# Driving terms of states 12 to 15 made with the tokens on the partitions, scaled by ScalarE and turned back by TensorE

## The reference

```python
def step(hst, inp):
    u_i, dt_i, b_i, c_i = inp
    dA = jnp.exp(dt_i[..., None] * A)
    hst = dA * hst + (dt_i * u_i)[..., None] * b_i[:, :, None, :]
    y = jnp.einsum('bkdn,bkn->bkd', hst, c_i)
    return (hst, y)
```

## Time and profile before

| what | value |
|---|---|
| median of 3 runs | 12155.8 µs (12155.32 to 12169.84) |
| span of the profiled execution | 12166.4 µs |
| VectorE busy | 11096.6 µs, 91% |
| GpSimd busy | 9763.2 µs, 80% |
| TensorE busy (matmuls) | 8645.9 µs, 71% |
| ScalarE busy | 7723.7 µs, 63% |

### The profile page before, as it was taken

The page is one execution under the profiler, slowest core; times in us unless marked ns, Lnnn a source line. Parts: engine busy times, 40 slices in busy tenths (PEclk is TensorE's granted clock), DMA queues, the critical chain, the costliest instruction groups (busy, mean ns, idle before and its releaser), DMA issues. The chain is left out here.

```text
span 12166.4 us, 118425 instructions
## 1 busy us (share of the span) xinstructions
PE 8645.9 (71%) x25368; PEld 2428.9 (20%) x25368; DVE 11096.6 (91%) x7359; ACT 7723.7 (63%) x11653; POOL 9763.2 (80%) x4212
## 2 busy tenths in 40 slices
PE   8866666666666666666666666666666666488888
PEld 2321111111111111111111111111111111133333
DVE  7769999999999999999999999999999999866565
ACT  6766666666666666666666666666666666455555
POOL 0029999999999999999999999999999999711210
PEclk9977777777777777777777777777777777698989
DMA  3358877887778887787877788778777888643441
GB/s 107 112 152 182 182 182 181 182 182 183 181 182 182 182 181 183 182 182 178 184 182 182 178 186 182 182 176 185 182 182 178 188 184 184 157 102 91 105 103 48
DMA packets 569247, 2013.70 MB, mean 166 GB/s; under 512 B 82135, under 2 KB 87031, under 8 KB 553975
## 3 DMA queue, kind: packets, MB, share of 16 engines
q1 hardware_dynamic: 565490, 2005.63, 71.1%
q10 hardware_dynamic: 3076, 0.97, 0.1%
...
## 5 line engine op out<-in xcount | busy, mean ns | idle before, releaser
L858 POOL TENSOR_TENSOR dBu<-rep,shared 128x1024 f32<-128x1024 f32 x3072 | 7165.7, 2363 | 837.4 <-DMA rep<-dd_dram 830.8
L641 PE MATMUL py<-hC,fold 128*32 128x512 f32 x12288 | 2966.4, 863 | 2450.5 <-POOL hC L865 1908.2
L818 DVE TENSOR_TENSOR_SCAN pd<-pd,dBu 128x1024 f32<-128x1024 f32 x2048 | 4670.5, 2281 | 16.5 <-issue 6.9
L689 ACT ACTIVATE pd<-rep,a_now 128x1024 f32<-128x1024 f32 x3072 | 3419.6, 1113 | 929.5 <-DVE hC L826 739.4
L826 DVE TENSOR_TENSOR hC<-pd,shared 128x1024 f32<-128x1024 f32 x2048 | 2507.5, 1224 | 160.0 <-DVE pd L818 26.3
L865 POOL TENSOR_TENSOR hC<-h,shared 128x1024 f32<-128x1024 f32 x1024 | 2408.1, 2352 | 242.1 <-DVE h L818 240.9
L818 DVE TENSOR_TENSOR_SCAN h<-pd,dBu 128x1024 f32<-128x1024 f32 x1024 | 2333.3, 2279 | 24.2 <-ACT pd L689 24.2
L701 ACT ACTIVATE carry<-pd 128x1 f32<-128x1 f32 x1536 | 262.0, 171 | 2072.0 <-DVE hC L826 2054.3
L641 PEld LDWEIGHTS py<-hC,fold 128*32 128x32 f32 x12288 | 522.8, 138 | 4666.8 <-POOL hC L865 2770.2
L610 PE MATMUL pp<-xdbl,w_dt 38*96 38x512 f32 x1024 | 714.8, 832 | 371.8 <-ACT xdbl L718 369.3
L599 PE MATMUL pp<-u,w_x 96*38 96x512 f32 x1024 | 670.0, 817 | 338.3 <-DVE RL L801 303.5
...
...
## 6 DMA issues: line engine op xcount, KB each, us to landing
rep<-dd_dram SPq DMA_DIRECT2D x1024, 768.0 KB, 12.1
shared<-bc_dram SPq DMA_DIRECT2D x2048, 256.0 KB, 8.8
u<-u_dram SPq DMA_DIRECT2D x128, 768.0 KB, 5.3
dd_dram<-LG SPq DMA_DIRECT2D x256, 384.0 KB, 4.8
dd_dram<-RL SPq DMA_DIRECT2D x256, 384.0 KB, 3.0
y_dram<-y SPq DMA_DIRECT2D x256, 384.0 KB, 11.6
...
```

The costliest lines, as they stand in the source:

```text
L641: last = mm(py[32 * g:32 * g + 32, t2(t)], fold[:, :], hC[:, j % 2 * 3 + g, t2(t)], start=(j % 4 == 0), stop=(j % 4 == 3), skip_group_chec ...
L689: go(pd[:, i % 2, :], rep[:, half, 0, g, :], ACT.Exp, scale=a_now[:, i:i + 1]).then_inc(S.exped, 1)
L818: v.tensor_tensor_scan(turned(dst, k), turned(pd[:, i % 2, :], k), turned(dBu[:, i % 4, :], k), 0.0, ALU.mult, ALU.add).then_inc(S.scanned, 1)
L858: nc.gpsimd.tensor_tensor(dBu[:, i % 4, :], rep[:, half, 1, g, :], BC[:, s, 0, r, :], ALU.mult).then_inc(S.dbu, 1)
```

## The change

Tiles of r = 3 get their dBu in another way, and are neither driven by GpSimd nor weighed by VectorE.

- The triples are put in another order: `TRIPLES` places both triples of r = 3 side by side, as tiles 9 to 14. Tiles 0 to 8 are r = 0 to 2 of the first half, tiles 15 to 23 r = 0 to 2 of the second.
- TensorE turns the rows of B (`turn_b`) and `delta*u` (`turn_du`) so that the tokens lie on the partitions, in eight blocks of 128. ScalarE copies them out (`copy_b`, `copy_du`), and multiplies each block with the B of its tokens, one state at a time, as a scale per partition (`scale_du`, 32 instructions on 128 x 192 a chunk). TensorE turns the products back (`turn_back`, eight transposes a tile) into a slot of `pd`.
- dA of those tiles goes to `hs` in SBUF, three slots, and the scan runs there in place; the saved state is the scan's first value instead of a fold. All six are weighed by GpSimd, which drives 18 tiles a chunk instead of 24 and weighs 12 instead of 8. VectorE weighs 12 instead of 16.
- `hs`, the turned arrays and B and C share the space that held two copies of B and C. There is one copy of each now, loaded row group by row group (`load_b`, `load_c`, 28 transfers instead of 16).
- The small steps move: `absolute` to `log` of half 0 and of half 1 stand one to two turns earlier, `copy_delta` in turns 8 and 18 instead of 10 and 21, `delta_u` behind tiles 9 and 19 instead of 12 and 23, `copy_x_dbl` in turn 23, `copy_y` in turns 3 and 15. `turned` in names of the code also means "run backwards" (`turned(row, k)`), as before.

```diff
+        turned_dbu = a.shared[:, 0:6 * T].rearrange("p (q g j d) -> p q g j d", q=TB, g=6, j=J)
+        turned_du = turned_dbu[:, :, :, J - 1, :]
+        BB = a.shared[:, 6 * T:9 * T].rearrange("p (r t) -> p r t", r=3)
+        hs = a.shared[:, 9 * T:12 * T].rearrange("p (g t) -> p g t", g=3)
+        CC = a.shared[:, 12 * T:16 * T].rearrange("p (r t) -> p r t", r=4)
...
+        TRIPLES = ((0, 0), (0, 1), (0, 2), (0, 3), (1, 3), (1, 0), (1, 1), (1, 2))
+        DRIVEN, WEIGHED, TURNED, SCALED = 18, 12, 6, 4 * TB
...
+            def turn_du(m, half):
+                pe.wait_ge(S.delta_made, done(m * 2 + half + 1))
+                pe.wait_ge(S.du_made, done(m * 2 + half + 1))
+                for q in range(TB):
+                    last = nc.tensor.transpose(pp[:, q * 128:q * 128 + HALF], du[:, block_of(q)], eye)
+                last.then_inc(S.du_turned, 1)
+
+            def turn_back(bk, c, i):
+                half, r, g = where(i)
+                n = bk * NC + c
+                if where(i - 2)[1] < 3 and where(i - 2)[2] < 2:
+                    pe.wait_ge(S.hc_dve, done(weighed_dve(n, i - 2)))
+                    if c < NC - 1:
+                        pe.wait_ge(S.carried, done(carries(bk, c, i - 2)))
+                else:
+                    pe.wait_ge(S.scanned, done(scanned(n, i - 2)))
+                for q in range(TB):
+                    if i == 9:
+                        pe.wait_ge(S.scaled, done(n * SCALED + min(J * q + 7, SCALED)))
+                    last = nc.tensor.transpose(pd[:, i % 2, block_of(q)], turned_dbu[:, q, half * 3 + g, :, :],
+                                               eye128[:, :])
+                last.then_inc(S.dbu_turned, 1)
...
+            def scale_du(n, s, first, last):
+                for step in range(first, last):
+                    if step == 0:
+                        act.wait_ge(S.du_copied, done(n * 2 + 2))
+                        act.wait_ge(S.b_copied, done(n + 1))
+                        act.wait_ge(S.dbu_turned, done(n * TURNED))
+                    q, j = scale_order(step)
+                    if j == J - 1:
+                        act.wait_ge(S.scaled, done(n * SCALED + max(J * q + 2, 3)))
+                    go(turned_dbu[:, q, :, j, :], turned_du[:, q, :, :], ACT.Identity,
+                       scale=turned_b[:, s, q, j:j + 1]).then_inc(S.scaled, 1)
...
+            AHEAD = 8
+            SCALE = {0: 4, 1: 3, 2: 3, 3: 1, 4: 2, 5: 3, 6: 4, 7: 4}
+            SCALE_NEXT = {21: 2, 22: 4, 23: 2}
...
+                if r == 3:
+                    dve.wait_ge(S.exped, done(scanned(n, i)))
+                    dve.wait_ge(S.dbu_turned, done(n * TURNED + i - 8))
+                    first = 0.0
+                    if c > 0:
+                        dve.wait_ge(S.carried, done(carries(bk, c - 1, i)))
+                        first = carry[:, i:i + 1]
+                    v.tensor_tensor_scan(turned(hs[:, g, :], k), turned(hs[:, g, :], k), turned(pd[:, i % 2, :], k),
+                                         first, ALU.mult, ALU.add).then_inc(S.scanned, 1)
+                    return
```

More of the change, by code:

```diff
@@ L647, in _ @@
             make_x_dbl(0, 0)
-            make_step(0, 0)
-            add_up(0, 0)
-            make_step(0, 1)
-            add_up(0, 1)
+            turn_b(0)
+            for half in range(2):
+                make_step(0, half)
+                add_up(0, half)
+                turn_du(0, half)
             make_x_dbl(1, 1)
+            turn_b(1)
             def body(bk, k, c, left):
                 n, s = bk * NC + c, c % 2
-                for j in range(8):
-                    if left and j == 0:
-                        make_step(n + 1, 0)
-                    if left and j == 2:
-                        add_up(n + 1, 0)
-                    if left and j == 6:
-                        add_up(n + 1, 1)
-                    if left >= 2 and j == 7:
-                        make_x_dbl(n + 2, s)
-                    reduce_states(n, j)
-                    if j % 4 == 1:
-                        skip(n, s, j // 4)
-                    if left and j == 3:
-                        make_step(n + 1, 1)
+                if left:
+                    make_step(n + 1, 0)
+                reduce_states(n, 0)
+                reduce_states(n, 1)
+                skip(n, s, 0)
+                if left:
+                    add_up(n + 1, 0)
+                for i in (9, 10, 11):
+                    turn_back(bk, c, i)
+                reduce_states(n, 2)
+                turn_back(bk, c, 12)
+                if left:
+                    turn_du(n + 1, 0)
+                turn_back(bk, c, 13)
+                if left:
+                    make_step(n + 1, 1)
+                turn_back(bk, c, 14)
+                reduce_states(n, 3)
+                reduce_states(n, 4)
+                if left:
+                    add_up(n + 1, 1)
+                reduce_states(n, 5)
+                skip(n, s, 1)
+                if left:
+                    turn_du(n + 1, 1)
+                if left >= 2:
+                    make_x_dbl(n + 2, s)
+                reduce_states(n, 6)
+                if left >= 2:
+                    turn_b(n + 2)
+                reduce_states(n, 7)
             chunk_loop(pe, body)
@@ L730, in relu @@
                 act.wait_ge(S.dd_stored, done((m * 2 + half) * 32))
+                act.wait_ge(S.du_turned, done(m * 2 + half))
                 go(RL[:, :], pp[0:HALF, :], ACT.Relu, bias=b_dt[:, half:half + 1]).then_inc(S.relu_made, 1)
@@ L755, in _ @@
             copy_x_dbl(0)
+            copy_b(0, 0)
             for half in range(2):
-                for step in (absolute, exp_abs, relu, one_plus, log, copy_delta):
+                for step in (absolute, exp_abs, relu, one_plus, log, copy_delta, copy_du):
                     step(0, half)
```

311 lines of the change are left out of this document (209 added, 102 removed).

## The result

The changed kernel takes 13093.0 µs in the median (13085.3 to 13113.0, 4 runs), the kernel before 12155.6 beside it. The ratio is 1.0775, 95% interval 1.076 to 1.079: it is slower by 937 µs, where 884 were predicted. The profiled execution spans 13111.2 µs. `copy_x_dbl` (L859) runs once a chunk from 790.6 to 11366.6 µs, so a chunk lasts (11366.6 - 790.6) / 127 = 83.28 µs; before, the same line gives (10433.1 - 787.6) / 127 = 75.95. The difference of 7.33 µs times 128 is 938 µs, the whole loss. From 1000 to 10400 µs, within the scan of both, VectorE is busy 84% of the time, before 98%.

The account below looks back on a forecast made before the run. The scan was taken as bound by VectorE and GpSimd at once; -5.0 + 7.2 + 2.4 + 1.9 + 0.4 = +6.9 µs a chunk, 883 µs over 128 chunks, gave about 13040 µs, range 12510 to 13760.

Parts of the forecast that it names:

- VectorE's and GpSimd's work: Two triples become six scans: VectorE saves 5.0 µs a chunk; GpSimd goes from 32 operations to 30.
- The wait before tile 9: Tile 9's transposes queue on TensorE behind reduction 1, skip and add_up: 7.2 µs a chunk, 5.5 with reduction at full clock.
- Two of the prediction's own signs: Turned tiles' scans idle some 10 µs a chunk before them; add_up's last matmul ends 5 to 7 µs after VectorE falls idle.
- neither sign against it: Wrong if VectorE is busy over 95% of the scan, or scaled instead of add_up holds tile 9's transposes.
- ScalarE in front of it: Turns 0 to 7: scalings of 0.36 µs delay tiles 6 to 8 by up to 2 µs, hidden under tile 9's wait.
- The waits in tiles 12 to 14: Transposes must fit one scan; tile 14 waits 0.9 µs behind make_step at full clock; 6.2 together at half; 2.4 taken.
- The lean to the full clock: Tiles 12 to 14: TensorE expected mostly at full clock behind add_up, so 2.4 µs taken, against 6.2 at half.
- The wait at `delta_u` of half 1: After tile 19, copy_delta waits for add_up, two turns behind one_plus: 1.9 µs, 3.5 more if add_up starts at half clock.
- The rest: make_x_dbl waits for copy_du and stands before reduction 6, needed by the next chunk's tile 0: 0.4 µs a chunk.
- Half clock in the transposes: Rival, turned tiles: waits 6.2 instead of 2.4, delta_u 3.4; +5.5 µs a chunk more, 13750 µs; chance 0.18.
- The scalings took 0.44 µs, not 0.6: Rival: ScalarE bounds the front; scalings of 0.6 µs and more delay tile 5 by some 3 µs: 13400 µs; chance 0.08.
- No slower than before: Rival: TensorE at full clock from the second reduction, other waits vanish; decided at waits of 5.0 µs; 12150 µs; chance 0.07.

Follow-up runs that it names:

- e8: e7 with make_step of half 1 issued behind turn_back(14), absolute and exp_abs of half 1 a turn later: 12533.7 µs.
- e1: Changed kernel without the 48 turn_back transposes a chunk and the waits on them (output not the reference's): 12708.1 µs.
- e10: e8 with reduce_states(1) and skip of half 0 issued behind turn_back(10) instead of ahead of add_up: 12270.1 µs.
- e5: Changed kernel with copy_y of half 1 in ScalarE's turn 2 instead of 3: 13364.6 µs.
- e2: Changed kernel with the 32 scalings done once before the loop and not in it (output not the reference's): 13122.0 µs.
- e7: e5 and e4 together, plus add_up's additions of E and RL issued earlier and copy_y of half 0 in turn 14 instead of 15: 12788.2 µs.
- e4: Changed kernel with reduce_states(6) issued ahead of make_x_dbl instead of behind it: 12924.2 µs.
- e11: e10 with 11 instead of 8 of the 32 scalings done ahead in turns 21 to 23, fewer in turns 1 and 2: 12199.9 µs.

## Why the prediction was right, point by point

**VectorE's and GpSimd's work.** Right: 5.0 µs a chunk taken, 5.2 by the floor, which e8 bears out (tiles 9 to 15 in 14.5 with hardly a wait, where the floor has 14.4). The scan with the carry as its first value takes 2.330 µs, against 2.270 without.

**The wait before tile 9.** The mechanism was right: `add_up` stands before the transposes, and tile 9 waits for them (e1, e10). Tile 9 was predicted at 35.0 µs behind tile 0 (4983.8 - 4948.82) and came at 35.7. But this agreement is that of two errors. The step that took GpSimd's weighing of tile 5 as fixed relative to tile 0 failed: it came at 18.8 before (4967.65 - 4948.82) and comes at 22.4 in the chunk shown (5048.73 - 5026.35), in the mean at 19.0 and 21.0, since tile 0's weighing and tile 5's scan wait. And the chain behind it is shorter than taken, 14.2 µs (5062.92 - 5048.73), 14.6 in the mean, instead of 16.2, because reduction 1 runs in 1.92 and not 3.64: the end of the range that the prediction leaned away from. e5 shows both that this is worth some 2 µs a chunk and that it hangs on the late `copy_y`.

So the term itself was too large. VectorE, which comes to tile 9 late itself, waits 3.8 µs there and not 7.2, and what is missing is spent at tiles 0 to 6, in waits of 3.7 µs for which the sum had 0.4. The total of the sum came out near by luck in these two terms. Two of the prediction's own signs tell it: the scans of the turned tiles wait 4.9 µs a chunk for TensorE and not some 10, and the last matmul of `add_up` ends 2.8 µs after VectorE fell idle, in the mean, and not 5 to 7. The others came as said: `delta_u`, the length of the scalings, the chunk (83.3), and neither sign against it, since VectorE is busy 84% of the scan, and of the idle time before the transposes and their weight loads only 45.7 µs over the program end with a scaling.

**ScalarE in front of it.** The scaling lasts 442 ns, and four take 1.48, 0.35 from start to start where 0.36 was taken. e2 bears out that they cost nothing. What the prediction said of the delay itself, that it only moves tiles 6 to 8, is wrong in its place: the folds come late at tiles 4 to 6 already (1.7 µs in tiles 3 to 6, 1.3 of which e2 removes).

**The waits in tiles 12 to 14.** The sum was right, 2.3 against 2.4, and so was the place behind `make_step` (e8). It is spread otherwise than the value taken meant: tiles 12 and 13 do not wait, as at full clock, and tile 14 waits 2.75 in the chunk shown instead of 0.9, because `make_step` (2.98) and the transposes behind it (1.97) run at half clock in part. The lean to the full clock was right for the rest. Three windows of the changed kernel (length, busy PE, PEld, DVE, ACT, POOL, clock, DMA): over reduction 0, over the turned tiles up to `make_step`, and from there to behind tile 14's transposes:

```profile
5044.00:5051.00 7.00, 3.27 (x12) 0.59 (x12) 4.75 (x4) 6.58 (x12) 6.30 (x3) 0.57 0.31 94
5062.00:5073.00 11.00, 7.45 (x60) 5.11 (x58) 10.08 (x5) 6.64 (x11) 6.73 (x4) 1.00 0.41 116
5073.00:5080.00 7.00, 6.91 (x21) 2.82 (x24) 4.25 (x3) 3.94 (x7) 5.02 (x3) 0.56 1.04 208
```

The granted clock is 0.57 over the first, the lower level of 1.2 GHz for the most part, and 1.00 over the turned tiles, the upper level of 2.4 GHz, as it was over `add_up` before them. In the third it is 0.56, after TensorE had stood still for 1.07 µs before `make_step`. Eight transposes take 1.09 µs at the upper level, 0.117 apart, and 1.97 behind `make_step`, at the lower; tile 14's ran wholly at the upper level in 8% of the chunks, those of tiles 9 to 13 in 98% and more.

The Trainium skill, "TensorE: Matmul & The Clock Gate", section "Part 4: PE-mode transpose", says that the full clock does not engage for transposes. The trace does not agree for tiles 9 to 13, whose transposes ran at it; it had been granted before them, and whether transposes alone would raise or hold it no run here shows. The length of a single one, 295 ns in the mean, is near the page's 275, but they overlap, which decides here.

**The wait at `delta_u` of half 1.** 1.9 predicted, 2.5 measured; the mechanism is borne out (2.03 in the chunk shown, released by `copy_delta`). `one_plus` was the one start of `add_up` that the prediction counted; e7 shows a second, as late, reduction 4 behind `copy_y` of half 0.

**The rest.** This term was mis-sized. 0.4 was given to `make_x_dbl` before reduction 6, for a copy that it waits for; 2.0 came, because it waits for the load of `u`, which `skip` of half 1 holds back behind `add_up` (e4). The prediction asked where TensorE's queue is late for VectorE, and did not follow SyncE's wait on `skip` to the load and back into the same queue.

**The rivals.** Half clock in the transposes came at tile 14 alone. (Where the prediction speaks of "the third case below", this rival 2 is meant. It has 3.4 µs for `delta_u`, where the paragraph on that wait gives 1.9 and 3.5 more; by that its 13750 would be some 250 µs higher.) The scalings took 0.44 µs, not 0.6. No slower than before needed waits of 5.0 µs in sum; the changed kernel has 13.0, and e11, with all these steps moved, still has some 5.6 (76.4 - 70.8, the sum of the floor) over all chunks.
